# Expert weights resident in SBUF and addressed by register, in the experts stage of a graph and mixture network

## The reference

```python
xf = x.reshape(-1, D)                       # layer-normed nodes, D = 256
logits = xf @ router_w.T + router_b
idx = jnp.argmax(logits, axis=-1)           # one of E = 32
w1t = jnp.take(W1, idx, axis=0)             # 256 x 64 for each node
h = jax.nn.relu(jnp.einsum('nd,ndh->nh', xf, w1t) + jnp.take(b1, idx, axis=0))
w2t = jnp.take(W2, idx, axis=0)             # 64 x 256
out = jax.nn.relu(jnp.einsum('nh,nhd->nd', h, w2t) + jnp.take(b2, idx, axis=0))
```

## Time and profile before

| | |
|---|---|
| timed runs, median of 3 | 4422.07 us (4420.8 to 4436.18) |
| span of the profiled execution, first to last instruction | 3913.9 us |
| PE busy | 2817.2 us (72%) |
| DVE busy | 1759.8 us (45%) |
| ACT busy | 768.9 us (20%) |
| POOL busy | 2555.5 us (65%) |

### The profile page before, as it was taken

The page is one execution under the profiler, slowest core; times in us unless marked ns, Lnnn a source line. Parts: engine busy times, 40 slices in busy tenths (PEclk is TensorE's granted clock), DMA queues, the critical chain, the costliest instruction groups (busy, mean ns, idle before and its releaser), DMA issues. The chain is left out here.

```text
span 3913.9 us, 41587 instructions
## 1 busy us (share of the span) xinstructions
PE 2817.2 (72%) x12730; PEld 2139.6 (55%) x12730; DVE 1759.8 (45%) x4424; ACT 768.9 (20%) x1634; POOL 2555.5 (65%) x2689
## 2 busy tenths in 40 slices
PE   3577877777768647667777777665677777777778
PEld 2466656656544535556555555544466555556557
DVE  6433335555524842443333333332355555555533
ACT  1111101111103313321111111110122222222210
POOL 3677777777760342557777777775777777777701
PEclk9999988888879879889989999887889999999969
DMA  4344434444433457754444444433344444444405
GB/s 139 116 117 120 124 107 139 130 138 131 129 96 94 143 164 202 213 179 133 138 117 125 124 125 125 114 111 97 109 123 122 124 124 123 123 121 125 125 21 197
DMA packets 279533, 501.68 MB, mean 128 GB/s; under 512 B 59771, under 2 KB 179969, under 8 KB 279162
## 3 DMA queue, kind: packets, MB, share of 16 engines
q0 software_dynamic: 126240, 345.85, 30.9%
q1 hardware_dynamic: 135916, 139.10, 11.5%
q10 hardware_dynamic: 17136, 13.84, 1.1%
HBM read 419.12 MB, written 79.18 MB: 127 GB/s over the span
## 5 line engine op out<-in xcount | busy, mean ns | idle before, releaser
L1476 PE MATMUL bank<-g,m 128*128 128x256 f32 (+1 forms) x4704 | 1466.0, 436 | 806.4 <-DMA g<-d_t,src_i 537.4
L1399 POOL DMA_INDIRECT g<-d_t,src_i x1568 | 1505.2, 960 | 511.4 <-issue 511.4
L1476 PEld LDWEIGHTS bank<-g,m 128*128 128x128 f32 x4704 | 879.6, 211 | 1102.3 <-issue 400.1
L1399 POOL DMA_INDIRECT g<-d_xn,src_i x784 | 802.3, 1023 | 244.3 <-issue 242.5
L1424 DVE TENSOR_SCALAR m<-iota,rel_f,ew_f 128x128 f32<-128x128 f32 x1568 | 421.6, 365 | 255.9 <-PE bank L1476 250.4
L1440 DVE TENSOR_TENSOR accT<-bank,accT 128x256 f32 x294 | 122.8, 418 | 593.1 <-PE bank L1464 592.9
L1405 ACT ACTIVATE s<-bank 128x256 f32<-128x256 f32 (+1 forms) x294 | 111.4, 379 | 1076.0 <-PE bank L1478 554.7
L1427 DVE TENSOR_TENSOR eq<-iota,rel_f 128x1024 bf16<-128x1024 f32 x98 | 119.9, 1224 | 138.3 <-PE bank L1478 138.3
L1478 PE MATMUL bank<-ones_b,eq 128*128 128x1 bf16 x784 | 136.9, 175 | 0.0
L1340 PE MATMUL bank<-wg,side_lg 128*128 128x256 f32 (+1 forms) x392 | 132.1, 428 | 2.9 <-DVE side_lg L1332 2.9
L219 POOL TENSOR_TENSOR rsd<-ved,mhalf 128x2 f32<-128x2 f32 (+1 forms) x25 | 19.0, 760 | 175.6 <-DVE ved L213 175.4
(11 more groups left out here) (387 smaller groups left out, 4273.3 us busy)
## 6 DMA issues: line engine op xcount, KB each, us to landing
g<-d_t,src_i POOLq DMA_INDIRECT x1568, 2.8
side_xn<-d_xn SPq DMA_DIRECT2D x96, 256.0 KB, 3.1
g<-d_xn,src_i POOLq DMA_INDIRECT x784, 2.8
d_swT<-wkv SPq DMA_DIRECT2D x48, 256.0 KB, 3.0
swT<-d_swT SPq DMA_DIRECT2D x24, 512.0 KB, 3.8
xt<-d_xs POOLq DMA_DIRECT2D x80, 128.0 KB, 3.0
d_ys<-y ACTq DMA_DIRECT2D x80, 128.0 KB, 2.6
x<-in_x SPq DMA_DIRECT2D x24, 256.0 KB, 2.7
```

What stands on the lines that cost most here:

```text
L1399: pool.indirect_dma_start(g[n % RING][:, u, 0:D], None, table, bass.IndirectOffsetOnAxis(ap=k.src_i[:, t:t + 1], axis=0)).then_inc(gathere ...
L1476: ins = pe.matmul(b[:, 0:GW], m[o][:, u, :], g[r][:, u, :], start=(u == 0), stop=(u == GT - 1 and not count))
```

## The change

All 32 experts' first weights (2 MB, packed by row on the host) are loaded once into `k.dinv`, whose former content is loaded again only at the head of the Between pass; the biases lie behind them, and the second weights with their bias row lie in a new buffer `w2` of 65 partitions. The three loads are issued by SP at the head of the routing stage. To make room, `wfx` and `wout` are allocated later, and they too are loaded at the head of the Between pass. In the experts stage SP loads the tiles in place of POOL. A new class reads table entries eight at a time, on SP for the pages and on PE, DVE and ACT for the experts. DVE copies the expert's first weights from `k.dinv` into one of two small buffers, and the output product and the hidden bias are addressed by register in place.

```diff
@@ class of the Between pass's side task, SP
     def move(self, i, w):
+        if i == 0:
+            sp, k = self.e_sp, self.k
+            sp.dma_start(k.dinv[:, 0:N], bcast_rows(self.d.deg[0, 0:N], N)).then_inc(self.dinv_loaded, 16)
+            sp.dma_start(k.wfx[:], self.a["L1_ffn_W_fx"].rearrange("(c p) n -> p c n", p=P)).then_inc(self.late, 16)
+            sp.dma_start(k.wout[:], self.a["L1_ffn_W_out"].rearrange("(h c) n -> c h n", c=SDIM)).then_inc(self.late, 16)
         for n in (2 * i, 2 * i + 1):
...
         wait(dve, self.t_psum, i - 1)
+        dve.wait_ge(self.dinv_loaded, 16)
...
@@ stage_gnn_second, SP
-                    if i == 1:
-                        sp.dma_start(k.dinv[:, 0:N], bcast_rows(d.deg[0, 0:N], N)).then_inc(spread, 16)
-                sp.wait_ge(spread, 16)
...
+class TileNumbers:
+    AT_ONCE = 8
+    def __init__(self, nc, engine, row, most):
+        self.nc, self.engine, self.row, self.most, self.values = nc, engine, row, most, {}
+    def of(self, t):
+        n = t // self.AT_ONCE
+        if n not in self.values:
+            at = slice(n * self.AT_ONCE, min((n + 1) * self.AT_ONCE, SORTED))
+            self.values[n] = self.nc.values_load_multi_w_load_instructions(self.row[0:1, at], engines=[self.engine], min_val=0, max_val=self.most)[1]
+        return self.values[n][t % self.AT_ONCE]
...
@@ stage_route
+        w1 = k.dinv[:, 0:EXPERTS * 2 * HID]
+        b1 = k.dinv[0:HID, EXPERTS * 2 * HID:EXPERTS * (2 * HID + 1)]
+        w2 = st.sb("w2", [HID + 1, EXPERTS * D])
...
+                    sp.dma_start(w1, a["expert_in"]).then_inc(weights, 16)
+                    sp.dma_start(b1, a["expert_bias"]).then_inc(weights, 16)
+                    sp.dma_start(w2[:], a["expert_out"]).then_inc(weights, 16)
                     pipeline(sp, (load, 0), (store, 3))
+                    sp.wait_ge(weights, 48)
                     sp.wait_ge(tails_known, 1)
...
@@ stage_experts: POOL's block goes, SP's becomes
+                page = TileNumbers(nc, mybir.EngineType.SP, k.tile_page, EXPERTS * REGION - 1)
                 def load(t):
                     r = t % DEEP
+                    x = page.of(t)
+                    tails.landed(sp, t)
+                    wait(sp, turned, t - DEEP + 1)
+                    sp.dma_start(xt[r][:], pages[bass.ds(x, 1), :, :].rearrange("a p d -> p (a d)")).then_inc(x_loaded[r], 16)
...
@@ stage_experts, PE
-                    wait(pe, w_loaded[r], 16 * (t // DEEP + 1))
+                    wait(pe, w_copied, t + 1)
                     wait(pe, h_done, t - 1)
                     for c in range(C):
-                        ins = pe.matmul(k.bank[2 + j][:, 0:P], w1[r][:, c * HID:c * HID + P], xT[j][:, c, :], start=(c == 0), stop=(c == C - 1))
+                        ins = pe.matmul(k.bank[2 + j][0:HID, 0:P], mine1[j][:, c * HID:(c + 1) * HID], xT[j][:, c, :], start=(c == 0), stop=(c == C - 1))
...
+                    e = expert.of(t)
                     wait(pe, h_done, t + 1)
-                    wait(pe, v_loaded[r], 16 * (t // DEEP + 1))
                     wait(pe, y_done, t - 1)
-                    pe.matmul(k.bank[4 + j][:, 0:D], hT[j][:], w2[r][:], start=True, stop=True).then_inc(out_psum, 1)
+                    pe.matmul(k.bank[4 + j][:, 0:D], hT[j][0:HID + 1, :], w2[:, bass.ds(e * D, D)], start=True, stop=True).then_inc(out_psum, 1)
...
@@ stage_experts, DVE
+                def copy_w(t):
+                    e = expert.of(t)
+                    wait(dve, hid, t - 1)
+                    dve.tensor_copy(mine1[t % 2][:], w1[:, bass.ds(e * H2, H2)]).then_inc(w_copied, 1)
...
-                tiles(dve, (copy_xT, 0), (index, 0))
+                tiles(dve, (copy_w, 0), (copy_xT, 0), (index, 0))
...
@@ stage_experts, ACT
                 def relu_h(t):
-                    r, j = t % DEEP, t % 2
+                    j, e = t % 2, expert.of(t)
                     wait(act, hid, t + 1)
                     wait(act, out_psum, t - 1)
-                    act.activation(hT[j][0:HID, :], k.bank[2 + j][0:HID, 0:P], ACT.Relu, bias=w1[r][0:HID, H2:H2 + 1]).then_inc(h_done, 1)
+                    act.activation(hT[j][0:HID, :], k.bank[2 + j][0:HID, 0:P], ACT.Relu, bias=b1[:, bass.ds(e, 1)]).then_inc(h_done, 1)
```

More of the change, by code:

```diff
@@ L828, in __init__ @@
         k = self.k = st.kit
-        self.d = d
+        self.a, self.d = a, d
+        self.dinv_loaded, self.late = st.sem("side_spread"), st.sem("side_late")
         self.xn = [st.sb(f"side_xn{j}", [P, 2, D + 1]) for j in range(self.XN)]
@@ L901, in sp_end @@
             self.send(i)
+        sp.wait_ge(self.late, 32)
         for j in range(self.T):
@@ L1848, in stage_gnn_second @@
         stats = st.sb("stats", [P, C, NBLK, 6])
[L1849 removed]
+        h_done, u_done, kept, stat_done = (st.sem(s) for s in ("h_done", "u_done", "kept", "stat_done"))
         n_loaded = [st.sem(f"n_loaded{j}") for j in range(2)]
@@ L1954, in stage_route @@
         tails = Tails(st, k, d, zero)
+        w1 = k.dinv[:, 0:EXPERTS * 2 * HID]
+        b1 = k.dinv[0:HID, EXPERTS * 2 * HID:EXPERTS * (2 * HID + 1)]
+        w2 = st.sb("w2", [HID + 1, EXPERTS * D])
         with Stage(nc, kit) as sr:
+            weights = sr.sem("weights")
             xm = Slots(sr, "xm", [P, 2, D], dma="sp")
@@ L2182, in stage_experts @@
         start = st.sb("start", [P, NTILE])
-        x_loaded = [st.pool_dma(f"x_loaded{j}") for j in range(DEEP)]
-        w_loaded = [st.sem(f"w_loaded{j}") for j in range(DEEP)]
-        v_loaded = [st.sem(f"v_loaded{j}") for j in range(DEEP)]
+        x_loaded = [st.sem(f"x_loaded{j}") for j in range(DEEP)]
+        mine1 = [st.sb(f"mine1_{j}", [P, H2]) for j in range(2)]
+        w_copied = st.sem("w_copied")
         sent = [st.sem(f"y_sent{j}") for j in range(DEEP)]
@@ L2197, in stage_experts, with _ @@
         with nc.Block() as block:
-            @block.gpsimd
-            def _(pool):
+            @block.sync
+            def _(sp):
+                page = TileNumbers(nc, mybir.EngineType.SP, k.tile_page, EXPERTS * REGION - 1)
                 def load(t):
                     r = t % DEEP
[L2202 to L2206, removed]
-                for j in range(DEEP):
[L2208 to L2218, removed]
-                    sp.dma_start(w2[r][0:HID + 1, :], a["expert_out"][bass.ds(e, 1), :, :].rearrange("a h d -> h (a d)")).then_inc(v_loaded[r], 16)
-                tiles(sp, (load, 0))
+                    x = page.of(t)
+                    tails.landed(sp, t)
+                    wait(sp, turned, t - DEEP + 1)
+                    sp.dma_start(xt[r][:], pages[bass.ds(x, 1), :, :].rearrange("a p d -> p (a d)")).then_inc(x_loaded[r], 16)
+                tiles(sp, (load, 0))
+                for j in range(DEEP):
+                    sp.wait_ge(x_loaded[j], 16 * (SORTED // DEEP))
             @block.tensor
             def _(pe):
-                pe.wait_ge(padded, 2 * DEEP + 2)
+                expert = TileNumbers(nc, mybir.EngineType.PE, k.tile_expert, EXPERTS - 1)
+                pe.wait_ge(padded, 2)
                 def turn(t):
@@ L2252, in _ @@
             def _(dve):
-                for j in range(DEEP):
-                    dve.memset(w1[j][:, H2:C * HID + HID], 0.0).then_inc(padded, 1)
-                for j in range(DEEP):
-                    dve.memset(w2[j][HID:P, :], 0.0).then_inc(padded, 1)
                 for j in range(2):
                     dve.memset(hT[j][HID:P, :], 1.0).then_inc(padded, 1)
+                expert = TileNumbers(nc, mybir.EngineType.DVE, k.tile_expert, EXPERTS - 1)
+                def copy_w(t):
+                    e = expert.of(t)
+                    wait(dve, hid, t - 1)
+                    dve.tensor_copy(mine1[t % 2][:], w1[:, bass.ds(e * H2, H2)]).then_inc(w_copied, 1)
                 def copy_xT(t):
@@ L2668, in build @@
         k.wkv1 = sb("wkv1", [P, C, 2 * D])
-        k.wfx = sb("wfx", [P, C, 2 * D])
         k.wxs = sb("wxs", [P, C, 2 * D])
-        k.wout = sb("wout", [SDIM, HEADS, D])
         k.wslice = sb("wslice", [SDIM, SDIM])
@@ L2692, in build @@
         stage_route(nc, k, a, d)
+        k.wfx = sb("wfx", [P, C, 2 * D])
+        k.wout = sb("wout", [SDIM, HEADS, D])
         k.mq = k.w1T
```

17 lines of the change are left out of this document (7 added, 10 removed).

## The result

| | before | after |
|---|---|---|
| timed runs, median | 4426.82 us (4420.8 to 4436.18, 4 runs) | 4525.06 us (4506.98 to 4530.33, 4 runs) |
| ratio | | 1.0222, 95% interval 1.0181 to 1.0263 |

The changed kernel is 98 us slower; the prediction was 18 us. Its profiled execution spans 4528.4 us. The page of the kernel before shows a quicker execution (3913.9 us) than any of its timed runs, so I compare stages with a second profile of the kernel before, span 4351.1 us, taken with the first experiments. It has the same routing and experts stages as the earlier trace rows within 5 us; what was longer in it were the passes over the edges, which the change leaves alone.

What follows compares the result with a forecast made beforehand. The prediction took SyncE's pair of weight loads per tile, 1.9 us, to bound the experts stage, then a PE, ACT, PE ring. Experts +4 us and routing +14 us on 4422 us gave 4440 us, range 4412 to 4462.

Steps and rivals of the forecast that it cites:

- no gain: Experts stage: 64 stationary columns in place of 128 save nothing, since weight loads already lie beside the matmuls.
- 1.80 us and 3.7 us: Experts stage: time from ReLU to ReLU in a steady round, and in every eighth round, with its read of eight.
- the forecast's own sign of being wrong: Experts stage: the prediction is wrong if the steady round is 1.6 or over 2 us.
- PE's read: Experts stage: PE's read of eight makes it 1.3 us late, inside ACT's 1.9 us for the same tile.
- the prediction's 159: Experts stage: the ReLUs would run over some 159 us in the changed profile.
- the prediction's rate of 3.2 us per 1000 KB: Routing head: load rate taken from dinv's load; 4136 KB ahead of the first xm then take 13.1 us.
- rival C: Routing: the 65-partition load runs at half rate, 6.6 us more, routing +21, 4447 us; chance 0.10.
- the sum's 14: Routing: three loads ahead of the first xm delay it, passed on in full to the stage's end, +14 us.
- Between pass: right: Loads at its head make PE some 8 us late, covered by GpSimd's gathers; 0, with 0 to +8 us.
- The 508 us: Base: difference between the 3913.9 us span and the 4422.07 us median, taken to lie around the span, unaffected by the change.
- B's extra cost per read: Experts stage: reads add up, each of nine rounds 1.3 to 2 us more, 4452 to 4458 us; chance 0.20.
- D's hidden reads: Experts stage: SyncE's loads were the whole bound, all added work is hidden, -30 us, 4392 us; chance 0.06.

Runs made afterwards that it cites:

- f3: e2 with numbers read one at a time in place of eight; 4417.24 us against 4431.28 us, ratio 0.9970.
- e2: The changed kernel with full-width products and the second weights loaded behind the last xm; 4390.08 us against 4360.18 us, ratio 1.0058.
- e1: The kernel before with the inner product on 64 columns and the output product on 65 rows; 4402.61 us against 4360.18 us, ratio 1.0125.
- g1: The changed kernel with numbers read one at a time, both products still narrow; 4510.11 us, the kernel before 4421.48 us.
- g2: The changed kernel with single reads and the inner product at full width, the output product on 65 rows; 4529.86 us.
- h1: g1 with a warm-up of 24 extra full-width products ahead of TensorE's first tile; 4441.22 us.
- h2: g2 with a warm-up of 24 extra full-width products ahead of TensorE's first tile; 4451.12 us.
- i1: The changed kernel, narrow products and reads of eight, with only the 24-product warm-up added; 4552.83 us against 4410.72 us before.
- f2: The changed kernel with full-width products and second weights padded to 128 rows in DRAM, loaded where the change loads them; 4458.76 us.
- f4: The changed kernel at full width, weights in eight pieces, single reads but none on PE and ACT, GpSimd copying bias and second weights; 4412.73 us, ratio 0.9953.
- f1: The kernel before with the output product alone narrowed to 65 rows; 4428.14 us against 4431.28 us.
- e3: The kernel before with the inner product alone on 64 weight columns; 4361.08 us.
- h3: The changed kernel with single reads, output product at full width, inner product on 64 columns, no warm-up; 4419.05 us.

## Why the prediction was wrong

**The step that failed** is the sentence "The inner product's stationary has 64 columns in place of 128, but its weight loads already lie beside the matmuls; no gain", and the 65 rows of the output product, which it passed over. I priced the narrower products by what they do beside the matmuls, and took the round at the clock of the kernel before. They act on the clock. Full-width rounds rise out of half clock (f3: 1.00 from 12 us into the stage; e2: behind each of nine pauses); rounds with 65 rows didn't in e1, g1 and g2, though they hold full clock once there, as long as nothing pauses (h1, h2; i1 lost it). The experts stage begins at 0.50 in every kernel here. So the changed kernel stays there.

The size of it, by the experts stage alone: with single reads, narrow against full width is 240.2 against 154.3 us, 86 us (g1, f3); with reads of eight 249.5 against 189.4 or 187.8, some 60 us (e2, f2). In the kernel before the same two slices are 64 us (e1). "No gain" was too kind at full clock as well: h1 has the changed kernel's products and 1.91 us a round, against 1.78 with full width (h2), so the 64 columns cost 0.13 us, some 10 us over the stage. The reads of eight against single ones are 35 us at full width and 9 us at half clock, where PE's own longer round hides most of them.

**The round and the reads: right, but only with full-width products.** Predicted 1.80 us and 3.7 us. The changed kernel has 2.90 and 3.59; the forecast's own sign of being wrong, a steady round over 2 us, came true. In e2, with full width at full clock, they are 1.78 and 3.56. PE's read did lie inside ScalarE's: the ReLU that ended the pause was late by its own issue (2.93 us), and PE's output product followed 0.5 us behind it. 70 x 1.78 + 9 x 3.56 = 157 us between first and last ReLU, near the prediction's 159. But e2 shows 177.5 us: the remaining 21 us are rounds at half clock, 16 behind the pauses and 5 at the stage's start. The sum charged each pause once, for its own length; it has to be charged again for the clock.

**Routing: mechanism right, one term mis-sized.** The delay passes on nearly in full (first sum 18.5 us later, stage +16). `w1` and the biases cost 6.4 us (e2), as by the prediction's rate of 3.2 us per 1000 KB. The 65-partition load cost the other 12.1 us where the sum had 6.7; that was rival C's half rate, which I gave 0.10. The Trainium skill's "SBUF — State Buffer" (Door 1: The DMA port swizzle) says that partitions 0 to 63 reach half of the ports; by this, the trace agrees (packets of 2.39 us to 65 partitions and 1.21 us to 128). For the first sum rival C's 21 us was nearer than the sum's 14 (18.5 us late), for the length of the stage (+16) the sum was.

**Between pass: right.** The side product started 22 us after the stage's start in place of 9, and PE waited 6 us for it. The rest of the pass took it up: with the same loads e2's pass is no longer than that of the kernel before (1142 against 1145 us).

**The base.** The 508 us between the page and the timed runs lie within the span, not around it: spans of timed runs are some 2 us below their times. The core of that page had a mean granted clock of 0.897, that of the later runs of the same kernel 0.807 to 0.821; why it was quicker stays open. The sum of differences was not hurt by that, but the step was wrong.

**Rivals.** B's extra cost per read did not occur; D's hidden reads came true nearly whole once the numbers were read singly at full width (f3), and f4 has no reads on the ring. No rival had the clock, and the range ended 45 us below the changed kernel's fastest run.

**Open.** That the two narrow products kept the clock down is shown; why they do is not. Why 65 rows of contraction keep it from rising and 64 columns alone don't, and where between 65 and 128 it turns, wasn't tried. In f1 the clock did rise with the same 65 rows, in the shorter rounds of the kernel before (2.53 us at half clock, against 2.71 in g2), and with the 64 columns added (e1) it didn't. g1 to i1 are one execution each.

## What to carry to other kernels

Before taking zeros out of a product, look at the granted clock around it: a full-width product over padding may be what brings the clock up, and two slices cost 64 us of 163 in a kernel otherwise untouched. A pause on TensorE can be paid twice, once in its length and once in the rounds behind it (16 and 16 us in e2), so spread register reads singly behind work that covers them, and not in groups of eight. And a large load ahead of a stage's first input delays the whole stage; in pieces beside the work it cost next to nothing (f4), and to 65 partitions it ran at under half the rate of one to 128 (171 against 395 GB/s).

## What the hardware showed that I had not expected

- The granted clock depends on where it stood: identical rounds ran 2.90 us at 0.50 (g1) or 1.91 us at 1.00 (h1) for a whole stage. The Trainium skill's "TensorE: Matmul & The Clock Gate" (Part 1) lets the clock follow how busy TensorE has been; by the busy time of the trace, g1 doesn't agree (231 of 240 us busy at 0.50).
- A product with 64 weight columns made the round no quicker: rounds grew by 0.13 us at full clock, 1.60 to 1.73 us (e3) and 1.78 to 1.91 us (h3).
- A read of eight numbers into registers took 0.55 us on ScalarE and 0.59 us on TensorE (medians in e2), about twice a read of one (0.28 and 0.30 us in f3; the 0.53 us of the earlier trace rows was measured while the tails were filled); the eight checks and assertions behind it took the other 2.0 us of ScalarE's 2.57 between the issue of its store (1594.83 + 0.33) and the next ReLU (1597.73) in e2, 0.25 us a pair.
